# A macaron layer with routed experts on one core: who waits for the output weights' loads, who makes the input weights' low parts, and in which order the three products are taken

## What is computed

```python
def _L0_ffn_ref(layer_input, router_weight, w_in, w_out, bias):
    logits = (x @ router_weight.T).astype(jnp.float32)
    top_vals, top_idx = jax.lax.top_k(logits, TOP_K)
    top_gates = jax.nn.softmax(top_vals, axis=1).astype(x.dtype)
    ...
    def expert_step(acc, ew):
        wi, wo, g = ew
        h = x @ wi.T
        a, b = jnp.split(h, 2, axis=-1)
        o = jax.nn.silu(a) * b @ wo.T
        return (acc + g[:, None] * o, None)
...
x = x + 0.5 * _L0_ffn_ref(_layernorm(x, axis=-1), ...)
x = x + _L0_attn_ref(_layernorm(x, axis=-1), ...)
x = x + 0.5 * _L0_ffn_ref(_layernorm(x, axis=-1), ...)
```

## Time and profile before

| | |
|---|---|
| median of 3 runs | 463.65 us (461.63 to 465.14) |
| the profiled execution | 460.96 us, of which the span of its instructions is 459.2 us |
| busy: PE, DVE, ACT, POOL | 405.1, 306.8, 257.3, 267.0 us |

### The profile page before, as it was taken

The page is one execution under the profiler, slowest core; times in us unless marked ns, Lnnn a source line. Parts: engine busy times, 40 slices in busy tenths (PEclk is TensorE's granted clock), DMA queues, the critical chain, the costliest instruction groups (busy, mean ns, idle before and its releaser), DMA issues.

```text
span 459.2 us, 10279 instructions
## 1 busy us (share of the span) xinstructions
PE 405.1 (88%) x2912; PEld 332.1 (72%) x2913; DVE 306.8 (67%) x605; ACT 257.3 (56%) x638; POOL 267.0 (58%) x315
## 2 busy tenths in 40 slices
PE   6764097899999999888999999989689999999996
PEld 3433086787888887666878788766378888888885
DVE  6780089967565568688667767686745567565566
ACT  2700177655655654558878878762145555556552
POOL 5552059878655771876686767720155477655860
PEclk9598579999999999999999999999999999999999
DMA  7619931111122217000000000001772111112126
GB/s 265 240 43 334 390 126 35 47 58 57 46 63 51 57 42 256 1 1 0 5 1 0 0 0 0 0 2 48 235 245 61 58 48 57 57 57 57 46 69 229
DMA packets 25738, 38.89 MB, mean 85 GB/s; under 512 B 3056, under 2 KB 20720, under 8 KB 25712
## 3 DMA queue, kind: packets, MB, share of 16 engines
q1 hardware_dynamic: 19088, 24.41, 15.5%
q0 software_dynamic: 4544, 12.07, 9.0%
q10 hardware_dynamic: 2080, 2.10, 1.3%
HBM read 29.37 MB, written 9.19 MB: 84 GB/s over the span
## 4 chain that ended last, share of the span: by engine, by line
PE 59%; DVE 16%; issue 6%; SPq 6%; DMA 5%; ACT 3%; POOL 2%; DVEq 1%; ACTq 0%; POOLq 0%
PE bank L1309 22%; PE bank L1331 12%; PE bank L1466 6%; PE bank L1477 3%; PE bank L1319 3%; PE bank L1433 2%; DMA w_out<-y_scratch 2%; SPq L388 2%; SPq L397 2%; PE bank L1285 2%; PE bank L1513 2%; DMA y_scratch<-arena,scatter_row 1%; PE bank L1467 1%; DVE arena L871 1%; DVE v L1210 1%
## 5 line engine op out<-in xcount | busy, mean ns | idle before, releaser
L514 POOL DMA_INDIRECT arena<-xn_scratch,gather_row x46 | 53.9, 1173 | 56.4 <-PE bank L1285 32.9
L1004 DVE TENSOR_TENSOR wo_lo<-w_out,wo_hi 128x1024 fp32r<-128x1024 f32 x46 | 69.9, 1520 | 22.7 <-ACT wo_hi L679 18.7
L520 POOL DMA_INDIRECT y_scratch<-arena,scatter_row x42 | 58.2, 1385 | 29.0 <-ACT arena L690 24.4
L679 ACT ACTIVATE wo_hi<-w_out 128x1024 fp32r x46 | 48.8, 1060 | 27.6 <-SPq L394 19.2
L1309 PE MATMUL bank<-w_hi,xT_hi 128*128 x184 | 62.2, 419 | 1.5 <-ACT xT_hi L653 1.3
L1309 PE MATMUL bank<-w_hi,xT_lo 128*128 x184 | 57.9, 396 | 0.3 <-DVE xT_lo L993 0.3
L1309 PE MATMUL bank<-w_lo,xT_hi 128*128 x184 | 58.0, 396 | 0.0
L1009 DVE TENSOR_TENSOR gT_lo<-bank,gT_hi 128x512 fp32r<-128x512 f32 x46 | 31.7, 689 | 37.9 <-ACT gT_hi L668 37.8
L606 POOL TENSOR_TENSOR k_head<-k_hi,head_mask 128x256 fp32r<-128x256 f32 x64 | 38.7, 625 | 28.1 <-PE bank L1467 21.0
L661 ACT ACTIVATE arena<-bank 128x512 f32<-128x512 f32 x46 | 27.5, 598 | 46.5 <-PE bank L1309 46.5
L1331 PE MATMUL bank<-wo_hi,gT_hi 128*128 128x256 f32 x184 | 33.5, 305 | 17.6 <-ACT gT_hi L668 17.6
(11 more groups left out here) (181 smaller groups left out, 997.2 us busy)
## 6 DMA issues: line engine op xcount, KB each, us to landing
w_raw<-in_win_t SPq DMA_DIRECT2D x8, 1024.0 KB, 12.7
w_out<-in_wout_t SPq DMA_DIRECT2D x16, 512.0 KB, 7.3
w_out<-y_scratch SPq DMA_DIRECT2D x16, 256.0 KB, 4.6
xn_scratch<-arena ACTq DMA_DIRECT2D x2, 1024.0 KB, 6.7
x<-in_x SPq DMA_DIRECT2D x4, 256.0 KB, 3.8
out<-x SPq DMA_DIRECT2D x4, 256.0 KB, 2.1
arena<-xn_scratch,gather_row POOLq DMA_INDIRECT x46, 3.6
y_scratch<-arena,scatter_row POOLq DMA_INDIRECT x46, 3.0
```

Of the source, the lines that this page charges most:

```text
L514: pool.indirect_dma_start(out=xb[j % 2][:, :], out_offset=None, in_=xn_dram, in_offset=bass.IndirectOffsetOnAxis(ap=gather_row[:, j:j + 1] ...
L520: pool.indirect_dma_start(out=y_dram, in_=y[j % 2][:, :], in_offset=None, out_offset=bass.IndirectOffsetOnAxis(ap=scatter_row[:, j:j + 1], ...
L679: act.activation(wo_hi[u][:, :, :], w_out[:, bass.ds(e, 1), :, :].rearrange("p o c d -> p (o c) d"), ACT.Copy)\
L1004: dve.tensor_tensor(wo_lo[:, :, :], w_out[:, bass.ds(e, 1), :, :].rearrange("p o c d -> p (o c) d"), wo_hi[u][:, :, :].bitcast(F32), ALU.s ...
```

## The change

1. `pass_on_w_out` is not run for f = 0. In the first FFN ACT itself waits for `wout_loaded[j]`, the load of the expert numbered as the block, in `split_out`(j) for j < 8, and for none later. For f = 1 nothing changes.
2. So that j is a constant there, `PEELED` goes from 5 to 7, the loop from 8 to 7 rounds.
3. `split_back` is gone from POOL. DVE's `split_low`(e) makes both halves of `w_lo`. For expert 0 it moves from ahead of the routing to behind it, for experts 1 and 2 from the middle of the routing to between and behind the first `xT_lo`.
4. PE takes the three products in the order high by high, low tokens by high weights, high tokens by low weights; it waits for `w_hi`, `xT_lo` and `w_lo` each ahead of the product that reads it.
5. SP starts input weights 2 ahead of output weights 0, and input weights e ahead of output weights e-2 for e = 3 to 7.
6. `WARM_LN` adds 5 warm products behind the wait for the router's load and 1 a pair later.

```diff
-PEELED = 5
+PEELED = 7
...
+WARM_LN = (5, 1, 0, 0)
...
             load_w_in(1)
+            load_w_in(2)
             load_w_out(0)
-            load_w_in(2)
...
             for e in range(EARLY, E):
+                load_w_in(e)
                 load_w_out(e - EARLY + 1)
-                load_w_in(e)
...
-                if f == 0:
-                    pass_on_w_out(0)
-                else:
+                if f:
...
-                    if f == 0 and j == 2:
-                        split_back(2)
                     gather(f, j)
                 zero_rows(f)
                 for j in range(SCATTERED):
-                    if f == 0 and j + EARLY < E:
-                        split_back(j + EARLY)
...
-                act.wait_ge(wout_ready, e + (f * E + 1))
+                if f:
+                    act.wait_ge(wout_ready, e + 1)
+                elif isinstance(j, int) and j < E:
+                    act.wait_ge(wout_loaded[j], 16)
...
             def split_low(e):
-                dve.wait_ge(w_hi_ready, 2 * e + 1)
-                dve.tensor_tensor(w_lo[:, e, 0, :], w_raw[:, e, 0, :], w_hi[:, e, 0, :].bitcast(F32),
-                                  ALU.subtract).then_inc(w_lo_front, 1)
+                for half in range(DK):
+                    dve.wait_ge(w_hi_ready, DK * e + half + 1)
+                    dve.tensor_tensor(w_lo[:, e, half, :], w_raw[:, e, half, :], w_hi[:, e, half, :].bitcast(F32),
+                                      ALU.subtract).then_inc(w_lo_ready, 1)
...
-                for part, (tok, wts) in enumerate(((xT_hi, w_hi), (xT_hi, w_lo), (xT_lo, w_hi))):
-                    if half == 0 and part == 2:
+                for part, (tok, wts) in enumerate(((xT_hi, w_hi), (xT_lo, w_hi), (xT_hi, w_lo))):
+                    if half == 0 and part == 0 and f == 0:
+                        pe.wait_ge(w_hi_ready, e * DK + DK)
+                    if half == 0 and part == 1:
                         pe.wait_ge(xT_lo_ready, f * BLOCKS + j + 1)
+                    if half == 0 and part == 2 and f == 0:
+                        pe.wait_ge(w_lo_ready, e * DK + DK)
```

More of the change, by code:

```diff
@@ L251, in build @@
         w_hi_ready = sem("w_hi_ready")
-        w_lo_front = sem("w_lo_front")
-        w_lo_back = sem("w_lo_back")
+        w_lo_ready = sem("w_lo_ready")
         wout_loaded = [sem(f"wout_loaded{e}") for e in range(E)]
@@ L388, in load_w_out, with pass_on_w_out @@
                 sp.dma_start(w_out[:, e, :, :], wout_in[e].rearrange("(k p) n -> p k n", p=P)).then_inc(wout_loaded[e], 16)
-            def pass_on_w_out(f, experts=range(E)):
-                for e in experts:
-                    sp.wait_ge(wout_loaded[e], 16 * (f + 1))
+            def pass_on_w_out():
+                for e in range(E):
+                    sp.wait_ge(wout_loaded[e], 32)
                     sp.sem_inc(wout_ready)
@@ L424, in _ @@
                         load_w_out(e)
-                    pass_on_w_out(1)
+                    pass_on_w_out()
                 sp.wait_ge(slots_ready, f + 1)
@@ L496, in _ @@
             assert steps[0] == CONSTS
-            def split_back(e):
-                pool.wait_ge(w_hi_ready, 2 * e + 2)
-                pool.tensor_tensor(w_lo[:, e, 1, :], w_raw[:, e, 1, :], w_hi[:, e, 1, :].bitcast(F32),
-                                   ALU.subtract).then_inc(w_lo_back, 1)
             def add_bias(phase, b, first=0, pairs=TPAIRS):
@@ L550, in ffn @@
             def ffn(f):
-                if f == 0:
-                    split_back(0)
-                    pool.wait_ge(chosen_ready, 1)
-                    split_back(1)
                 pool.wait_ge(plan_ready, f + 1)
@@ L881, in split_low @@
             def split_low(e):
-                dve.wait_ge(w_hi_ready, 2 * e + 1)
-                dve.tensor_tensor(w_lo[:, e, 0, :], w_raw[:, e, 0, :], w_hi[:, e, 0, :].bitcast(F32),
-                                  ALU.subtract).then_inc(w_lo_front, 1)
+                for half in range(DK):
+                    dve.wait_ge(w_hi_ready, DK * e + half + 1)
+                    dve.tensor_tensor(w_lo[:, e, half, :], w_raw[:, e, half, :], w_hi[:, e, half, :].bitcast(F32),
+                                      ALU.subtract).then_inc(w_lo_ready, 1)
             def route(f):
-                if f == 0:
-                    split_low(0)
                 for n, tiles in enumerate((range(TILES - 2), range(TILES - 2, TILES))):
@@ L969, in route @@
                     .then_inc(scatter_ready, 1)
-                if f == 0:
-                    for e in range(1, EARLY):
-                        split_low(e)
                 dve.wait_ge(e1_ready, f + 1)
@@ L1072, in ffn @@
                 route(f)
+                if f == 0:
+                    split_low(0)
                 copy_xT_low(f, 0, 0)
+                if f == 0:
+                    split_low(1)
                 copy_xT_low(f, 1, 1)
@@ L1077, in ffn @@
                 split_out_low(f, 0, 0, first)
+                if f == 0:
+                    split_low(2)
                 def body(j, u, gate_next=True, copy_next=True):
@@ L1294, in project @@
                     pe.wait_ge(xT_hi_ready, f * BLOCKS + j + 1)
-                    if f == 0:
-                        pe.wait_ge(w_lo_front, e + 1)
-                        pe.wait_ge(w_lo_back, e + 1)
                     if after_first(f, j, 2):
@@ L1371, in ffn @@
                             score_experts(0, (pair - 1,))
+                        warm(WARM_LN[pair])
                 else:
```

## The result

The changed kernel takes 438.84 us, the median of 4 runs (437.27 to 441.33), where the kernel before took 462.68 in the runs beside it (461.63 to 465.14). The ratio is 0.948, interval 0.942 to 0.9545. The profiled execution took 439.45 us, 437.4 of them its span.

A forecast was written before the change was run, and what follows sets the result against it. Three stretches bound the first FFN: routing to first gather, ACT's wait for SP's signal, then five bodies on DVE. Savings 3.5 + 17.2 + 4.7 = 25.4 us, so 463.65 - 25.4 = 438.2; 8-in-10 range 432 to 446.

The forecast's parts named there:

- Routing: Start to PE's turn of block 0: scores 0.9 us earlier, `choice` and the cast 1.5, turn at 27.4, 3.5 earlier.
- Gather and loads: First FFN: gather 1 stretched by 1.1 us beside `split_low`(0), so SP's loads start at about 29.7 in place of 32.29.
- Turn to first `gT_lo`: First FFN, block 0's turn to first `gT_lo`: 9.8 us in place of 27.0, 17.2 less, `gT_lo`(0) at 37.2.
- The template: Second FFN, where ACT doesn't wait for SP: `wo_lo`(0) 6.35 us behind the turn, carried over to the first FFN.
- First body: First FFN, `gT_lo`(0) to `gT_lo`(1) at 44.2: 7.0 us, ACT waiting for input weights 3 until about 37.0.
- the five: First five bodies of the first FFN: 7.0, 5.7 and three at 5.1, sum 28.0 us, 4.7 less.
- the 444: Rival: gathers bound the bodies under the loads, three bodies each lose 2 us: 444, chance 0.14.
- the 449: Rival: POOL's DMA instructions block DVE, up to 1.1 us each, 11 in five bodies: 449, chance 0.09.
- TensorE's clock: Rival: PE stays at half clock from short gaps between 37 and 65 us; fifteen bodies would end at 512, chance 0.02.
- the kinder case: Rival: input weights 3 land before 35 and warm products are hidden, 2.5 to 4 us more gained: 435 to 434, chance 0.12.
- the change does what it says: Rival denied this: first `wo_hi` waits as long for its own load, only 8.2 us gained: 455.4, chance 0.01.
- Costed at nothing: Put at zero: `PEELED` 7, `xT_lo` in second place, later output weights, gathers under the loads; attention and later bodies taken as unchanged.

The follow-up runs named there:

- early split: The changed kernel with `split_low`(2), the low part of expert 2, made ahead of the second `xT_lo`: 439.64 us, ratio 0.947 to the kernel before.
- second profile: The kernel before, run and profiled once more with nothing changed: 460.78 us.
- wait alone: The kernel before with only ACT's own wait for the output weights in the first FFN and `PEELED` 7: 446.11 us, ratio 0.965.

## Why the prediction was right, and where it was not

The time, 438.2 forecast and 438.84 measured, and its main claim hold: one wait, that for SP's signal, held the first FFN, and taking it away is most of the gain. That the two times lie within 0.7 us is in part luck: the gain is 23.8 by the medians, 1.6 less than the forecast 25.4, and the kernel before took 462.68 where the forecast started from 463.65, which hides 1.0 of it. By the prediction's own steps:

- **Routing: 3.5 forecast, 2.98 measured.** `choice` 0.26 and the cast 0.17 came as forecast. The warm products were hidden wholly, not by two thirds, and the scores even got shorter (1.91 against 3.21): `chosen` was ready 2.5 earlier. But the step left out what stands next: the 18 warm products, started earlier and in part at the lower clock, took 6.57 and made the plan's product late, 0.90 of idle time on DVE. The turn came at 27.92 for 27.4. This is the execution's more than the kernel's: in the early split's, with the same program up to there, the eighteen took 5.20, DVE waited 0.20, and the turn came at 27.15, 3.75 earlier than before. One more piece was left out: POOL started the first gather 1.05 behind its list, against 0.48 before (24.87 behind 23.82, 26.89 behind 26.41); no run says why.
- **Gather and loads.** SP began at 29.59, forecast 29.7. But both first gathers took 1.24 on POOL, where the earlier trace rows had 2.23, and the second of them ran wholly beside the pair of `w_lo` (26.41 to 27.64, the pair 25.59 to 27.94). The traces show what the row alone did not: in all twelve, such an instruction that starts within a subtraction ends 0.8 to 1.1 us behind the end of that one, and the next of the pair doesn't count. The second gather started 0.4 ahead of the end of the first subtraction; the one of the earlier trace rows started 1.1 ahead; a scatter in the first body (36.18, 0.2 into a subtraction) took 1.91. That time from the subtraction's end is about as long as the whole instruction takes alone. So there is a stretch, against the inference in the Trainium skill, "SBUF — State Buffer", section "Who interferes with whom", that descriptor work is spared, but it was smaller than the one carried over. That SP's start came out right is the late gather (24.87 for 24.5) and two small stretches in place of one large: luck in part.
- **Turn to first `gT_lo`: 9.8 forecast, 11.46 measured.** The template was taken from the second FFN, where TensorE runs at full clock. Here the first pair of products took 1.42 (0.76 in the second FFN) and the granted clock from 28 to 40 us was 0.86, from 28 to 34 0.72; the second `xT_hi` came 5.96 behind the turn. In the early split's execution, which had the full clock there, it came 4.37 behind it: 1.6 of the 1.7. The step that failed is the carrying over of a duration without its clock.
- **First body: 7.0 forecast, 5.13 measured; the five: 28.0 and 26.2.** The loads set the first body less than I said, because the body began 2.2 later, at 39.38, while input weights 3 were there by ACT's `w_hi` at 37.25 and output weights 1 held ACT for 0.49. The early split shows the other side: when `gT_lo` is early, the body takes 8.6. The second `gT_lo` came at 44.51, forecast 44.2, by the chain that was forecast (ACT's `w_hi` at 37.25 for 37.0). So the two misses, 1.7 and 1.8, cancel for a reason: whichever is late, the loads or block 0's chain, takes the other's slack. The bodies behind it took 5.38, 5.18, 5.36 and 5.17, forecast 5.7 and 5.1.
- **The sum.** At the tenth `gT_lo` 25.36 us earlier, forecast 25.4. As a size of the gain this flatters. The profiled execution of before had an unlucky first FFN, 2.1 longer than its second profile, and a lucky end of the attention; from profile to profile the gain is 21.5 (460.96 to 439.45). The time is the better judge: 23.8 us by the medians, 5.2% (4.55% to 5.8%), against 25.4.
- **Rivals.** No PE wait for a gather stands in the bodies (the 444 is out); no DVE subtraction was longer than 1.23 beside POOL's DMA instructions, `w_lo` pairs were 2.35 throughout (the 449 is out, and with it what the rule of the Trainium skill, "SBUF — State Buffer", section "SBUF: two separate sides", would give if descriptor work read SBUF). The 3.99 of a later `wo_lo`, at 77.04, stands beside POOL's addition of the bias, not beside a DMA instruction. TensorE's clock was 1.00 from 35 to 65. Of the kinder case the warm products came true, the loads by 35 were not seen, and the time isn't its 435. The first `wo_hi` started 0.9 behind the second `xT_hi`, so the change does what it says; at 34.76 it is later than the 32 to 34 forecast.
- **Costed at nothing** and not so: the end of the attention. It lost 2.7 us against the first profile of before, and by the second profile about 1.2. The slice from 46 to 57 us that the prediction read as empty on four engines had ACT's first `wo_hi` at its end, which changes nothing in the argument.

What each part is worth at the sixth `gT_lo`, when it alone is undone: the wait 20.7, POOL's halves 6.7, the warm products 2.9, the products' order 1.2 (nearly all of it not its own, as shown above), the loads' order 0.8 (about 1.5 with the turn of block 0 taken out). They sum to 32.3 where all together gave 25.0, or 22.9 by the second profile of before; the wait and POOL's halves alone sum to 27.4, so they cover for each other. Of the three small ones only the warm products' 2.9 is above what one execution differs from the next by (up to 1.3 at the turn of block 0). In time only the first two stand out: the wait's ratio lies clear of the changed kernel's interval, that of POOL's halves overlaps its upper end (458.46 and 443.19 us).

## What to carry to other kernels

When one engine signals for another that a load has landed, ask what else that engine must issue first: here the signal was 19 us late for data that had been there all along, and the consumer's own wait on the load was all it took. Behind such a stall the next limits stand close together (POOL's subtractions, loads, the clock), so a part's worth alone and its worth undone last are two numbers, and both belong in the sum. And a duration that is carried over from a later stage is only good with its granted clock beside it; one profile of a kernel can be 2 us off in a stage, which a second profile of the unchanged kernel shows.

## What the runs showed of the hardware

- A subtraction on DVE of 1.22 us took 2.1 to 4.1 when POOL did one at the same time, and POOL's 2.4 to 3.4. DVE's ended 1.1 us behind POOL's in all 21 such pairs of the traces in which it ended last, also where it stood first in the record (wait alone: 51.21 to 55.28, POOL's 51.77 to 54.18). Both on DVE take 2.35 us.
- POOL's DMA instructions took 0.94 to 1.02 alone. One that started within a subtraction of DVE ended 0.8 to 1.1 us behind the end of that subtraction (changed kernel: scatter 52.20 to 53.75 in the one from 51.67 to 52.89; before: gather 26.89 to 29.13 in the one from 26.81 to 28.02), so it took up to 2.2 us. DVE's were not stretched by them (2.35 for a pair in both cases).
- Six warm products took 1.46 us at a granted clock of 1.00 and 2.62 at the lower level. The falls at the end of the attention came in one execution of the kernel before and not in another, with the same program; what decides it stays open. The loss between the first FFN and the second, against the first profile of before, was 0.1 us (the wait alone), 1.2 (POOL's halves), 1.5 (the kernel before again), 2.7 (changed) and 3.5 (early split).
- 1.5 MB more of weights, started ahead of a store of 1 MB, took its landing from 8.2 (7.6 to 10.5 in other executions) to 13.3 us, and the gather waited for it; 1 MB started behind the store, while the routing was still on, delayed nothing.
